# A causal attention network on one core: one wait per maximum step on VectorE, and fewer settles

## What is computed

```python
q, k, v = heads(x @ W_query), heads(x @ W_key), heads(x @ W_value)
scores = jnp.einsum('bhqd,bhkd->bhqk', q, k)
scores = jnp.where(causal[None, None], -jnp.inf, scores)
scores = scores + alibi_bias(H, t, scores.dtype)[None]
scores = scores / jnp.sqrt(jnp.asarray(DH, scores.dtype))
w = jax.nn.softmax(scores, axis=-1)
ctx = jnp.einsum('bhqk,bhkd->bqhd', w, v).reshape(b, t, H * DH)
return ctx @ W_proj + b_proj
```

## Time and profile before

| | |
|---|---|
| median of 3 runs | 3156.91 us |
| the runs | 3158.53, 3156.91, 3149.24 us |
| the profiled execution | 3162.98 us |
| its span, first to last instruction | 3161.1 us |
| TensorE busy | 2660.9 us (84%) |
| VectorE busy | 2348.1 us (74%) |
| ScalarE busy | 1744.1 us (55%) |
| GpSimd busy | 871.3 us (28%) |
| L1310, maxima of whole blocks | 1040 x 684 ns |
| L1314, add-and-maximum | 2090 x 520 ns |

### The profile page before, as it was taken

How to read it: one execution, slowest core, us unless ns; L and a number is a source line. 1 busy time by engine, 2 the same in 40 slices (tenths; PEclk the granted TensorE clock), 3 DMA queues, 4 the chain that set the end, 5 groups by cost and what they waited for, 6 DMA issues and landing times.

```text
span 3161.1 us, 68949 instructions
## 1 busy us (share of the span) xinstructions
PE 2660.9 (84%) x19315; PEld 1133.9 (36%) x19315; DVE 2348.1 (74%) x7303; ACT 1744.1 (55%) x3500; POOL 871.3 (28%) x971
## 2 busy tenths in 40 slices
PE   5588888987888898888888888898888889888886
PEld 3233333342333333333333333334334333333333
DVE  3777868867676886868778786886877688686865
ACT  1265555646656564555656555564665656455563
POOL 3122242232212224242112324223221222424211
PEclk8699989999999999999999999999999989999998
DMA  3313031031213113021131302103121310302121
GB/s 100 79 47 93 5 86 37 26 93 40 69 36 89 41 33 93 2 76 43 53 80 47 85 9 81 45 26 93 40 70 39 90 36 33 93 3 84 34 69 53
DMA packets 130000, 177.88 MB, mean 56 GB/s; under 512 B 26366, under 2 KB 71060, under 8 KB 129600
## 3 DMA queue, kind: packets, MB, share of 16 engines
q1 hardware_dynamic: 129610, 173.23, 19.6%
HBM read 126.70 MB, written 45.38 MB: 54 GB/s over the span
## 4 chain that ended last, share of the span: by engine, by line
PE 49%; DVE 21%; issue 15%; DMA 6%; SPq 4%; ACT 3%; POOL 2%; DVEq 1%; ACTq 0%; POOLq 0%
PE big L1479 10%; PE ctx_ps L1556 8%; PE big L1538 8%; PE small L1515 8%; PE big L1468 6%; DVE small L1314 6%; PE big L1593 5%; DMA parts_dram<-region 3%; DVE stats L1262 3%; DVE mx L1314 3%; DVE mx L1310 2%; DVE region L1367 2%; POOL region L1054 1%; SPq L940 1%; PE big L1584 1%
## 5 line engine op out<-in xcount | busy, mean ns | idle before, releaser
L1095 ACT ACTIVATE probs<-big 128x512 f32<-128x512 f32 (+2 forms) x2560 | 1241.7, 562 | 592.3 <-PE big L1538 589.3
L1314 DVE CUSTOM_DVE_ANT_0 small<-small,mask 128x128 f32<-128x128 f32 (+3 forms) x2090 | 969.3, 520 | 370.2 <-PE small L1515 359.4
L1003 POOL TENSOR_SCALAR_AFFINE_SELECT probs<-probs 128x512 f32<-128x512 f32 x512 | 334.3, 657 | 1663.6 <-ACT probs L1095 1663.6
L1538 PE MATMUL big<-stack_q,stack_k 64*128 64x512 f16 (+3 forms) x6144 | 706.5, 330 | 99.4 <-ACT probs L1095 44.6
L1310 DVE TENSOR_REDUCE mx<-small 128x1 f32<-128x512 f32 x1040 | 665.0, 684 | 144.5 <-PE small L1515 139.4
L1515 PE MATMUL small<-stack_k,stack_q 64*128 64x512 f16 (+3 forms) x3130 | 482.3, 343 | 265.4 <-DVE mx L1314 197.9
L1556 PE MATMUL ctx_ps<-probs,v_ones 128*17 128x512 f32 (+3 forms) x6144 | 635.3, 499 | 5.6 <-ACT ctx_u L1105 4.8
L1538 PEld LDWEIGHTS big<-stack_q,stack_k 64*128 64x128 f16 x6144 | 248.0, 95 | 499.8 <-issue 433.5
L1515 PEld LDWEIGHTS small<-stack_k,stack_q 64*128 64x128 f16 x3130 | 141.3, 94 | 786.6 <-issue 764.5
L1314 DVE DVE_READ_ACCUMULATOR2_ANT mx<- 128x1 f32 x2090 | 294.2, 141 | 0.4
L1468 PE MATMUL big<-hT,w_qkv 128*128 128x512 f32 x544 | 277.9, 634 | 18.4 <-ACT probs L1095 15.8
(11 more groups left out here) (95 smaller groups left out, 2125.0 us busy)
## 6 DMA issues: line engine op xcount, KB each, us to landing
parts_dram<-region SPq DMA_DIRECT2D x136, 256.0 KB
stack_q<-parts_dram SPq DMA_DIRECT2D x134, 128.0 KB
stack_k<-parts_dram SPq DMA_DIRECT2D x268, 64.0 KB
stack_k<-parts_dram SPq DMA_DIRECT2D x134, 128.0 KB
stack_q<-parts_dram SPq DMA_DIRECT2D x268, 64.0 KB
w_qkv<-wqkv SPq DMA_DIRECT2D x17, 768.0 KB, 4.9
x_res<-x SPq DMA_DIRECT2D x36, 256.0 KB, 3.0
out<-x_res SPq DMA_DIRECT2D x36, 256.0 KB, 2.2
```

Of the source, the lines that this page charges most:

```text
L1003: g.affine_select(out=diag, in_=diag, compare_op=ALU.is_ge, fill=0.0, base=0, pattern=[[0, GH], [1, P]], channel_multiplier=-1).then_inc(m ...
L1095: s.activation(probs[:, n % HELD, heads, q0:], big[:, at.slot(turn), 0:len(pairs) * width] .rearrange("p (h q) -> p h q", h=len(pairs)), A ...
L1314: ins = v.tensor_tensor_reduce(out=held, in0=held, in1=mask[:, BANK - width:], scale=1.0, scalar=3.0 * NEG, op0=ALU.add, op1=ALU.max, accu ...
L1538: last = te.matmul(big[:, at.slot(at.turn() + parity), j * width:(j + 1) * width], stack_k[rows, c, g * PAIR_N + pair, kt * P:(kt + 1) * P ...
```

## The change

VectorE waits once per `max` step, for both banks, where it waited for each bank at its turn. It settles once, ahead of both banks, when the step's first piece lies on the diagonal; before, it settled in each bank. The releases stay one per bank. In `slot_order` the loop leaves as soon as `follow()` has emptied every list.

```diff
@@ -418,6 +418,8 @@
 
     while any(queues.values()) or later or joins:
         follow()
+        if not (any(queues.values()) or later or joins):
+            break
         options = []
@@ -1300,21 +1302,22 @@
                 if kind == "max":
                     _, _, g, pair, pieces = item
+
+                    dve.wait_ge(s_filled, at.now("max", 2))
+                    if pieces[0][0] // 4 <= pieces[0][1]:
+                        settle(dve)
                     for parity in range(2):
-                        dve.wait_ge(s_filled, at.now("max", 1 + parity))
-                        for n, (qt, blk, col) in enumerate(pieces):
+                        for qt, blk, col in pieces:
                             width = piece_width(qt, blk)
                             held = small[:, at.small(parity), col:col + width]
                             to = mx[:, g % 2, (parity * PAIR_N + pair) * NT + qt, blk:blk + 1]
                             if qt // 4 > blk:
-                                ins = v.reduce_max(to, held, AX)
+                                last = v.reduce_max(to, held, AX)
                             else:
-                                if n == 0:
-                                    settle(dve)
-                                ins = v.tensor_tensor_reduce(
+                                last = v.tensor_tensor_reduce(
                                     out=held, in0=held, in1=mask[:, BANK - width:],
                                     scale=1.0, scalar=3.0 * NEG, op0=ALU.add, op1=ALU.max, accum_out=to)
-                        ins.then_inc(s_freed, 1)
+                        last.then_inc(s_freed, 1)
```

## The result

The changed kernel takes 3178.32 us, the median of 17 runs (3163.93 to 3189.96). The kernel before has 3156.68 us in 17 runs beside it (3141.59 to 3167.45). The ratio is 1.0068, with a 95% interval of 1.0052 to 1.0084: slower by 0.7%, 21.6 us by the medians. The forecast was 3158.4 with 3171 as its upper end. The time lies above it, and beside the far price of rival (b), 3178.5.

The account below looks back on a forecast made before the run. The prediction took the loop of TensorE's fills and VectorE's releases of `small` as the bound, with no engine full. Removed waits at 0 plus 1.5 us of lateness on 3156.9 gave 3158.4 us, range 3146 to 3171.

Parts of the forecast that it names:

- rival (b): First bank's later start paid nearly everywhere in the loop: 3178.5 at 31 ns, 3167.4 at 15 ns; chance 0.10.
- What bounds the kernel: No engine is full; TensorE and VectorE wait for each other over `small`, in 437 and 261 places.
- a start over 0.20 us behind the pair: Sign in the later profile: VectorE starting that late after the pair of matmuls would make the slower rival right.
- The removed waits and settles at 0: At the second bank, 1173 waits and 653 settles go; hidden behind VectorE's work, they were taken to save 0.
- Rival (a): VectorE's settles not all hidden, so faster: 3147 if one in ten was exposed, 3127 if three; chance 0.10.
- bound of 98 us on the side of gain: Most the change could gain on VectorE: 653 removed settles at 0.15 us each.
- 0.25 us at 128 columns: Spacing of VectorE starts within a bank, 1511.11 to 1511.36, cited as showing the same as the equal 0.38 us.
- The lateness of the first bank, 8 ns: VectorE's first-bank start waits for the second matmul, 4 ns later at full clock, up to 31 slow; 8 ns taken.
- How many of them count, 261 x 0.7 = 183: Lateness counted at TensorE's 261 waits for VectorE's release, 70% of it by share of the chain: 1.5 us.
- rival (c): TensorE's clock falls elsewhere, either side: 3151 or 3166; chance 0.18, half to each side.
- 7.7 us for a point of the span at the lower level: Price of one span point more or less at TensorE's half speed: 31.6 us, 49% on the chain, half lost.
- The order of items: The new `break` in `slot_order` changes nothing; the order of items is the same.

Follow-up runs that it names:

- the control: Kernel before with a settle added at the second bank of the 520 steps that open with a reduction; 3156.53 us, ratio 1.0011.
- the late wait alone: Kernel before, but the first bank's wait asks for both banks; the second bank's wait and settle stay; 3172.67 us against 3149.40, ratio 1.0078.
- two settles: Kernel before with a second settle behind the first, at the first bank of steps that open with an add-and-maximum; 3188.29 us, ratio 1.0113.
- the small operation: Kernel before, with an 8-column add carrying the wait instead of a settle at the first bank of 653 add-and-maximum steps; 3194.08 us, ratio 1.0136.

## Why the prediction was wrong

- *What bounds the kernel.* The loop of fill, first bank and release was named as the place, and the runs bear that out both ways (1.0078 and 0.9921). Of the signs that the prediction gave, the one for rival (b), a start over 0.20 us behind the pair, came true at 0.21 us.
- *The removed waits and settles at 0.* Right. Crossing the parity still takes 0.38 us in the changed kernel, with no wait between:

```profile
1527.50 0.43 DVE L1317 CUSTOM_DVE_ANT_0 small<-small,mask 128x256 f32<-128x256 f32 x1 [0.68 <-PE small L1518]
...
1527.85 0.47 DVE L1317 CUSTOM_DVE_ANT_0 small<-small,mask 128x256 f32<-128x256 f32 x1
...
1528.23 0.47 DVE L1317 CUSTOM_DVE_ANT_0 small<-small,mask 128x256 f32<-128x256 f32 x1
...
1528.61 0.46 DVE L1317 CUSTOM_DVE_ANT_0 small<-small,mask 128x256 f32<-128x256 f32 x1
```

The starts 1527.85 to 1528.23 are the crossing, 1528.23 to 1528.61 stays within a bank, as in the earlier trace rows. Rival (a) is out, by this, by the control and by the late wait alone. The bound of 98 us on the side of gain was too wide, as it took 0.15 us for a settle from two different operations; ahead of one and the same operation, a reduction, it is 0.112. The 0.25 us at 128 columns showed nothing either way: it is a start within a bank, with no crossing beside it.

- *The lateness of the first bank, 8 ns.* This step failed. It put the second signal 8 ns behind the first, out of 4 ns at full clock and 31 at the slow one. It is 35 ns at both clocks: where the pair lasts 0.61 us, the starts moved by 34 and 34 ns too (medians 38 to 72 and 190 to 224). In the prediction's own sum that makes 261 x 35 ns x 0.7 = 6.4 us in place of 1.5. I took the end of a matmul for the arrival of its signal. The ends of matmuls are modelled, as the page says, and what counts is when the waiting engine moves. The Trainium skill has the same in "Perfetto Trace Analysis", "Per-engine timelines": TensorE's reported end is computed and not observed, and the signal comes after it. The trace agrees: the first increment is recorded 14 ns behind its matmul's reported end. The rest lies between the increments, as 26 ns went away when one was left out and the matmuls stayed. I should have taken the missing row, the cost of a second increment, as unknown and kept a wider bound.
- *How many of them count, 261 x 0.7 = 183.* This was too few, and is the second step that failed: 21.6 us / 35 ns is 617 full places. The counts came from rows that hold only idle times of over 0.15 us. The trace of before has 921 close starts and 519 fills within 0.25 us of a release, where the earlier trace rows have 437 and 261. With 35 ns in rival (b)'s 437 + 261 places it would have been 24.4 us. Its 31 ns gave 21.6 us, the measured difference, by luck: 31 ns is the spacing of the matmuls' ends at the slow clock, and most of the time is at the full one. And places can't be counted at one price: the diagonal steps carry nearly all, 476 x 35 ns = 17 us of lateness for 0.68%, some 21 us, and the reductions 445 x 35 ns = 16 us for 0.05%.
- *The clock.* The prediction took it as a separate rival (c) and put nothing for it into the sum. It moves along with the loss. In the runs of the experiments' kernel before the mean clock was 0.935 to 0.936, in the changed kernel's 0.928, in the late wait's 0.930, with two settles 0.930, with the small operation 0.925, and without TensorE's settle 0.936. In the profiled executions TensorE was at its lower level for 428 us before and 468 us after the change, while the time at full clock fell from 2733 to 2710 us. From run to run of one kernel, 0.01 less goes with some 21 us more; the prediction's 7.7 us for a point of the span at the lower level would have made it 15. By that slope, as an estimate, 0.008 of clock goes with 17 of the changed kernel's 27 us and 0.006 with 13 of the late wait's 23, and some 10 us are left in each. That is near (212 + 157) x 35 ns = 13 us, the lateness in the places where a fill follows the release. So more than half of the loss goes with the clock. The late wait is behind the whole, clock included, since the kernel with the late wait alone loses as much as the changed one; how it lowers the granted clock, no run here shows.
- *The order of items.* It stayed, as said: all engines' data operations are the same in number and order.

## What to carry to other kernels

Before merging two waits into one, ask which of them lies in a loop between two engines: a wait asked for while the engine is busy is free, and the merged one delays the start that isn't. Read the delay of a signal from the start of the engine that waits for it, not from the end of the instruction that sends it. And to win time in such a loop, look at the other engine's side of it as well, and take nothing for a gain that costs the full engine its own time. A shift of some tens of ns has no fixed price: compare the granted clock of the two kernels before counting nanoseconds.

## What the runs showed that I had not expected

- Two increments of one semaphore by two matmuls that end 4 ns apart let a waiter for both start 35 ns after a waiter for the first would, and the semaphore's events lie 34 ns apart; at full clock, one increment of 2 by the second matmul brings it to 9 ns behind a single one's (43 and 34 ns from that matmul's end).
- A settle between a wait and an operation costs 112 ns ahead of a reduction (149 for 37 ns) and 93 ns as a second one ahead of an add-and-maximum (282 for 189); on TensorE 89 ns (146 for 57). Behind a busy engine it costs nothing measurable.
- Moving some 470 starts by 35 ns cost 0.68% (0.46 to 0.89), and moving 445 others by as much cost 0.05% (-0.16 to 0.27). In a kernel with TensorE's settle gone, moving both sets cost 0.16%, with overlapping intervals.
- More than half of the loss goes with the granted clock: 0.936 to 0.928 between the kernels, at some 21 us for each 0.01 from run to run.
